# Segment attention on one Trainium2 core: the last sum of the rotary turn shared between GpSimd and VectorE

## The reference, cut to what matters

```python
def rope(t):
    z = t.reshape(t.shape[:-1] + (-1, 2))
    rh = jnp.stack([-z[..., 1], z[..., 0]], axis=-1).reshape(t.shape)
    return t * cos + rh * sin
q, k = (rope(q), rope(k))
...
scores = jnp.einsum('bhid,bhjd->bhij', q, kf) * DH ** (-0.5)
probs = jax.nn.softmax(scores, axis=-1)
o = jnp.einsum('bhij,bhjd->bhid', probs, vf)
...
x = x + jax.nn.silu(g) * a @ ff_w2 + ff_b2
```

## Time and profile before

| | |
|---|---|
| median of 3 runs | 1438.62 us (1436.42 to 1440.64) |
| the profiled execution | 1435.06 us, span 1433.3 us |
| busy in the span | PE 1186.2 us (83%), VectorE 1008.1 (70%), ScalarE 744.6 (52%), GpSimd 730.5 (51%) |
| GpSimd sines L1087 | 64, 83.0 us together |
| GpSimd sums L1090 | 64, queries 32 with 41.5 us and keys 32 with 40.5 us |
| chain that ended last, by engine | GpSimd 10% of the span, TensorE 9%, VectorE 5% |

### The profile page before, as it was taken

One profiled execution on the slowest core, in us unless ns is written; L12 is line 12 of the kernel. 1 busy time (PEld: TensorE's weight loads), 2 busy tenths in 40 slices (PEclk: granted clock), 3 DMA queues, 4 the chain that ended last, 5 costly groups with the idle time before them and its releaser, 6 DMA issues. The chain is left out here.

```text
span 1433.3 us, 38489 instructions
## 1 busy us (share of the span) xinstructions
PE 1186.2 (83%) x15852; PEld 760.5 (53%) x15852; DVE 1008.1 (70%) x1819; ACT 744.6 (52%) x1021; POOL 730.5 (51%) x1047
## 2 busy tenths in 40 slices
PE   3888836898989999999999999897496977869784
PEld 2555523555555555555556565554343746347472
DVE  5677765787888888888888787876456373774733
ACT  2333332567676767666676767675333425234150
POOL 2345648646455555555464646420068394783940
PEclk9999957999999999999999999999987999989995
DMA  7100013232313132313132222110000000000000
GB/s 177 49 0 0 0 33 120 79 100 66 112 59 112 64 109 69 109 56 121 58 99 80 95 83 86 58 49 20 16 0 2 1 7 3 0 6 0 6 0 6
DMA packets 70383, 75.66 MB, mean 53 GB/s; under 512 B 21308, under 2 KB 64956, under 8 KB 70108
## 3 DMA queue, kind: packets, MB, share of 16 engines
q1 hardware_dynamic: 70236, 73.58, 16.7%
HBM read 32.91 MB, written 0.92 MB: 24 GB/s over the span
## 5 line engine op out<-in xcount | busy, mean ns | idle before, releaser
L916 DVE TENSOR_REDUCE tops_sb<-ps_b 112x2 f32<-112x1000 f32 x384 | 460.0, 1198 | 130.2 <-PE ps_b L777 130.0
L878 ACT ACTIVATE probs_sb<-ps_a 128x896 f32<-128x896 f32 x352 | 322.6, 916 | 91.5 <-PE ps_a L758 91.5
L749 PE MATMUL ps_d<-probs_sb,values_sb 128*32 128x112 f32 x6144 | 226.8, 265 | 1.0 <-ACT probs_sb L878 1.0
L777 PE MATMUL ps_b<-keys_sb,queries_sb 64*112 64x500 f16 x768 | 162.6, 419 | 69.2 <-DVE tops_sb L916 63.7
L217 POOL TENSOR_SCALAR context_sb<-context_sb,ln_sb 125x128 f32<-125x128 f32 x384 | 166.4, 450 | 7.9 <-POOL ln_sb L235 7.8
L226 POOL TENSOR_TENSOR ln_sb<-st_sb 125x12 f32<-125x12 f32 x32 | 7.2, 223 | 308.4 <-DVE st_sb L960 283.0
L749 PEld LDWEIGHTS ps_d<-probs_sb,values_sb 128*32 128x32 f32 x6144 | 134.1, 109 | 40.2 <-issue 6.7
L758 PEld LDWEIGHTS ps_a<-queries_sb,keys_sb 64*128 64x128 f16 x3072 | 123.7, 103 | 52.4 <-ACT probs_sb L878 9.0
L777 PEld LDWEIGHTS ps_b<-keys_sb,queries_sb 64*112 64x112 f16 x768 | 49.6, 124 | 186.9 <-DVE tops_sb L916 120.9
L758 PE MATMUL ps_a<-queries_sb,keys_sb 64*128 64x112 f16 x3072 | 139.8, 210 | 6.2 <-ACT probs_sb L878 6.0
L1087 POOL TENSOR_TENSOR turn_b_sb<-turn_b_sb,const_sb 128x512 f32<-128x512 f32 x64 | 83.0, 1297 | 98.0 <-DVE turn_b_sb L1422 98.0
(11 more groups left out here) (253 smaller groups left out, 2019.3 us busy)
## 6 DMA issues: line engine op xcount, KB each, us to landing
keys_sb<-k_split_sb SPq DMA_DIRECT2D x288, 125.0 KB, 3.0
context_sb<-in_ctx SPq DMA_DIRECT2D x32, 750.0 KB
queries_sb<-q_split_sb SPq DMA_DIRECT2D x24, 112.0 KB, 5.5
keys_sb<-in_ones SPq DMA_DIRECT2D x3, 375.0 KB, 4.8
w_qk_sb<-in_w_qkv SPq DMA_DIRECT2D x1, 1024.0 KB, 11.5
queries_sb<-shift_sb SPq DMA_DIRECT2D x64, 1.8 KB
x_all_sb<-in_x SPq DMA_DIRECT2D x2, 448.0 KB
queries_sb<-in_zeros SPq DMA_DIRECT2D x8, 112.0 KB, 5.5
```

The source lines that it names most:

```text
L749: last = nc.tensor.matmul(o_bank[32 * (g % 4):32 * (g % 4) + 32, 112 * (g // 4):112 * (g // 4) + 112], values[r][:, k, g, :], probs[k % 2] ...
L777: last = nc.tensor.matmul(ps_b[0:2 * T, 512 * e:512 * e + 500], queries_of(b + d, e, g), keys[(r + d) % 3][64 * e:64 * e + 64, g, 500 * u: ...
L878: nc.scalar.activation(probs[s % 2][:].rearrange("p (e n) -> p e n", e=2), halves(ps_a[:, :]), ACT.Exp).then_inc(Q["probs_ready"], 1)
L916: nc.vector.tensor_reduce(tops[(b + d) % 2][:, :, n // 3, n % 3], ps_b[0:2 * T, :].rearrange("p (e n) -> p e n", e=2)[:, :, 0:500], axis=A ...
```

## The change

Of the odd slices, the sum of turn_a and turn_b is taken from GpSimd and given to VectorE. GpSimd still does all 16 sines, and the sums of the even slices. VectorE does the sum of slice n - 2 right behind the shuffle of each odd n from 3 on (ahead of gate and bias instructions that stand at the same n), and the sum of slice 15 behind the whole loop, after y and ahead of the first maximum. The counter rotated now counts the eight even slices and a new one, summed, the eight odd ones; whoever waited for rotated waits for the one or the other, and TensorE, ahead of the scores, for both.

```diff
@@ -1010,7 +1010,7 @@
             gate_e = sb3("gate_e", [128, 3, U * 128])
             y = sb3("y", [128, U, C])
 
-            per3 = dict(turn_done=16, turn_read=16, sines=16, rotated=16, v_done=2 * NB, v_ready=2 * NB, s_done=2 * U,
+            per3 = dict(turn_done=16, turn_read=16, sines=16, rotated=8, summed=8, v_done=2 * NB, v_ready=2 * NB, s_done=2 * U,
                         s_read=U, s_top=U, s_copied=U, s_shifted=U, e_ready=U, sum_ready=U, e_normal=U, et_done=2 * U,
                         et_ready=2 * U, o_done=2 * U, o_ready=2 * U, up_done=3, gate_tanh=3, up_ready=3,
                         out_done=U)
@@ -1037,6 +1037,11 @@
 
                 return n // 4 % 2, n % 4 + 4 * (n // 8)
 
+            def rotated_of(n):
+
+                kind, j = slice_of(n)
+                return k1[:, j, :, 0:TP] if kind else q1[:, j, :].rearrange("p (b t) -> p b t", t=TP)
+
             def scores1(u):
 
                 return (ps_a, ps_b)[u % 2][:, :].rearrange("p (r n) -> p r n", r=2)[:, :, 0:SC].rearrange(
@@ -1081,13 +1086,13 @@
                             return
                         for n in range(16):
                             wait("turn_read", n + 1)
-                            kind, j = slice_of(n)
-                            dst = k1[:, j, :, 0:TP] if kind else q1[:, j, :].rearrange("p (b t) -> p b t", t=TP)
+                            dst = rotated_of(n)
                             a, b = turn_a[n % NTURN], turn_b[n % NTURN]
                             nc.gpsimd.tensor_tensor(b[:], b[:], sin.unsqueeze(1).broadcast_to([128, NB, TP]), ALU.mult
                                                     ).then_inc(R["sines"], 1)
-                            wait("sines", n + 1)
-                            nc.gpsimd.tensor_tensor(dst, a[:], b[:], ALU.add).then_inc(R["rotated"], 1)
+                            if n % 2 == 0:
+                                wait("sines", n + 1)
+                                nc.gpsimd.tensor_tensor(dst, a[:], b[:], ALU.add).then_inc(R["rotated"], 1)
 
                         def normalise(u):
                             wait("sum_ready", u + 1)
@@ -1195,7 +1200,8 @@
                             pe.wait_ge(persist_ready, 1)
                             pe.wait_ge(loaded_v, 16 * NB)
                         for half in range(2):
-                            wait("rotated", 8 + 8 * half)
+                            wait("rotated", 4 + 4 * half)
+                            wait("summed", 4 + 4 * half)
                             for u in range(U):
                                 if half == 0:
                                     if u < 2:
@@ -1411,16 +1417,24 @@
                             link, ends = chain(ve, main_chain, i * NMAIN, NMAIN)
                             link(nc.vector.tensor_copy(k1[:, :, :, TP:NKM],
                                                        mem_k[:].rearrange("p j (i b) -> p i j b", b=NB)[:, i, :, :].unsqueeze(3).broadcast_to([128, NJ, NB, NM])))
+                        def add_turned(n):
+
+                            wait("sines", n + 1)
+                            nc.vector.tensor_tensor(rotated_of(n), turn_a[n % NTURN][:],
+                                                    turn_b[n % NTURN][:], ALU.add).then_inc(R["summed"], 1)
+
                         for n in range(16):
                             if attention:
                                 ps = banks[n % 4].rearrange("p (b t) -> p b t", t=TP)
                                 wait("turn_done", n + 1)
                                 if n >= NTURN:
-                                    wait("rotated", n - NTURN + 1)
+                                    wait("summed" if n % 2 else "rotated", (n - NTURN) // 2 + 1)
                                 nc.vector.tensor_tensor(turn_a[n % NTURN][:], ps, cos.unsqueeze(1).broadcast_to([128, NB, TP]),
                                                         ALU.mult)
                                 ins = nc.vector.stream_shuffle(turn_b[n % NTURN][:], ps, [p ^ 1 for p in range(32)])
                                 ins.then_inc(R["turn_read"], 1)
+                                if n % 2 == 1 and n >= 3:
+                                    add_turned(n - 2)
                             for part in range(2):
                                 if mlp and n - 1 - part in UP_AT:
                                     gate(UP_AT.index(n - 1 - part), part)
@@ -1436,6 +1450,7 @@
                                 mlp_ends()
                         if not attention:
                             return
+                        add_turned(15)
 
                         def total(u):
                             wait("e_ready", u + 1)
```

## The result

| | before | after |
|---|---|---|
| median | 1438.01 us (11 runs, 1433.88 to 1440.64) | 1443.16 us (11 runs, 1441.74 to 1449.62) |
| ratio | | 1.0051, 95% interval 1.0033 to 1.0068 |
| profiled execution, span | 1435.06, 1433.3 | 1449.62, 1447.8 |

The change makes the kernel slower by 0.5%: 5.2 us by the medians, 7.3 by the ratio. The forecast was +4.6 us and 1443.2. In a second comparison of the same two kernels, further down, the ratio was 1.0047 (1.0026 to 1.0068) and the medians 6.8 apart.

What follows compares the result with a forecast made beforehand. GpSimd was taken as the bound, VectorE with the gates close behind. Three gated passes at +1.9 (+5.6) and the first pass at -1.0 gave +4.6 us on 1438.62: 1443.2 us, 8-in-10 range 1435 to 1449.

Steps and rivals of the forecast that it cites:

- Price of an addition: Each sum moved to VectorE: 0.61 us beside an idle GpSimd, up to 1.82 when waiting for GpSimd's instruction.
- Slices 0 to 5: Start of a gated pass: additions wait for GpSimd, so slice 4 starts 2.9 us late and slice 6 3.73.
- Period behind: Gated pass from slice 6: four slices cost 9.30 us against 10.47; two groups give 2.35 back, slice 14 +1.38 late.
- First clock term: Second gate matmuls on TensorE: 5.3 us idle drops them to half clock, +1.92 us per gated pass, bounds 0 and 2.9.
- Second clock term: Down projection on TensorE: idle shrinks from 2.48 to about 1.3 us, clock returns, -1.7 us per gated pass.
- rule of nearness to the 1.66 that had left the clock full: Down projection: idle of about 1.3 us, below the 1.66 seen harmless before the gate matmuls, was taken as full clock.
- Sum of slice 15 in gated passes: Last moved addition, between y and the first row maximum: +0.28 us per gated pass.
- First pass: Pass without gates: GpSimd's gain mostly lost to row maxima queued behind VectorE's last addition, -1.0 us, bounds -2.4 and 0.
- same waits, better clock: Rival: second gate matmuls stay at 2.4 GHz, -1.92 us in each of three passes, 1437.4 us; chance 0.31.
- The additions aren't held: Rival: additions cost VectorE 0.61 us each and GpSimd nothing, 1427.0 us; chance 0.16.
- Slower still: Rival: turn matmul also at half clock (+1.0), down projection stays slow (+1.7), +2.7 us a pass, 1451.3 us; chance 0.08.

Runs made afterwards that it cites:

- e4: Changed kernel with TensorE multiplying slice 8 four more times into the same bank in gated passes; 1437.08 us, 1.0012 of the kernel before.
- e9: Changed kernel measured and traced once more without an edit; 1443.84 us, 1.0047 of the kernel before.
- e6: Kernel before, no sum moved, with TensorE multiplying slice 15 twice more in gated passes; 1432.07 us, 0.9965 of the kernel before.
- e1: Changed kernel with VectorE's odd sums reading one input from PSUM, placed ahead of the shuffle; 1426.98 us, 0.9943 of the kernel before.
- e10: Changed kernel with odd sums ahead of the shuffle, but both inputs in SBUF; 1445.93 us, 1.0062 of the kernel before.
- e11: Changed kernel with VectorE's bias addition moved from slice 3 to behind slice 7; 1445.97 us, 1.0054 of the kernel before.

## Why the prediction was right

The direction, the median (1443.16 for 1443.2) and the mechanism were right; that the median fell so near is luck in part, since single passes and the stages ahead vary by more. Step by step:

- *Price of an addition.* 0.67 to 1.75 measured, 0.61 to 1.82 taken. Alternation was right: 1.74 and 1.75 in a row.
- *Slices 0 to 5.* +2.92 at slice 4 for +2.9, +3.79 at slice 6 for +3.73. These hold in every gated pass.
- *Period behind.* From slice 10 to 14, 9.37 for 9.30. In e4, where the clock is full, both groups give back 1.1, for 1.17 summed.
- *First clock term.* The idle time was 5.08 (5.3 forecast). I took +1.92, only the two gate products slow. Measured against e4 at slice 10 it is 2.2, 2.5 and 2.5 us in the first trace, since part or all of the turn matmul (1.58 and 1.91 in place of 1.02) was slow too, and 2.0, 2.5 and 1.3 in e9's. The term was undersized, by about 0.25 on the mean of the six; 2.9 was its upper bound.
- *Second clock term.* -1.7 taken, -1.6 measured (e6, and 2.94 for 4.57 in after). The rule of nearness to the 1.66 that had left the clock full held, with 1.38.
- *Sum of slice 15 in gated passes.* +0.28 taken; between third gate and first maximum 5.22 for 6.60, of which 1.63 is the down projection: +0.25.
- *First pass.* -1.0 taken, -0.97 at the fifth maximum. But the sum had no term for what follows: only 0.33 of it was left at the next h in this trace; in e9's it was 1.54 at the maximum and 1.20 at the next h.
- *Not in the sum.* In the third and fourth pass of the first trace the step from first to fifth maximum was 0.7 longer, by scores at half clock; in e9's trace it was 7.43 or 7.44 in all three. With the first clock term it makes those two passes +3.3 where +1.9 was forecast; e9's are +2.1, +2.6 and +2.0. The total is 8.5 and 5.5 us in the two traces where 4.6 was forecast.

Of the rivals, "same waits, better clock" is what e4 makes by hand: 1.5 us over the kernel before by the medians, where it was priced 1.2 under. "The additions aren't held" is e1: 8.6 us under, where it was priced 11.6; one SBUF input brings it about, two don't. "Slower still" came in part: the turn matmul slow, the down projection not. The Trainium skill's rule on two SBUF inputs (SBUF — State Buffer, Who interferes with whom) is borne out, 1.74 beside 0.69. The Trainium skill's ratio for the two engines, 1.96 (GPSIMD Engine Reference, Elementwise side-by-side cycle accounting), is near that of the instructions here (0.69 for 1.27, 1.84) and was no guide to the kernel's time.

Left open: what sets how many instructions fall to half clock in a given pass, and why the stages ahead vary by 6 us between executions. Neither was tried. The length of the idle time alone doesn't settle it: behind 2.00 us the down projection of e10 took 4.57 twice and 2.94 once, and behind 3.1 us the second gate products L1169 of e1 took 2.08, 1.13 and 1.96.

## What to carry to other kernels

An elementwise instruction moved from GpSimd to VectorE doesn't cost its own length if both its inputs lie in SBUF and GpSimd stays busy: count it as up to GpSimd's instruction plus its own, and count what is queued behind it. Look where the moved instructions make TensorE wait and where they shorten a wait, since an idle time that grows past the ones the trace shows as harmless can be paid twice, and a few useless matmuls into a bank that isn't reported yet can win it back. Give a spare engine the work only in the pass where its queue has room, and put the last piece behind what doesn't need it, unless it fills a gap where it stands.

## What the runs showed that was not expected

Repeating finished work made the kernel faster in two places: two more matmuls of 0.86 us ahead of an idle time of 2.48 cut the down projection from 4.57 to 2.94 (e6, 0.9965 of the time), and four more took some 5 us off the changed kernel (ratios 1.0012 for e4, 1.0051 and 1.0047 for the changed kernel, in separate comparisons). And parting two instructions of VectorE that meet GpSimd didn't help: in e11 the waits turned up again within four slices, 1.74 and 1.75 at other places.
